# Graph convolution with split adjacency: all four chunks of adj and adjT split, none multiplied whole

## The reference

```python
HW = einsum('bnf,rfo->rbno', h, W[:, :F]) + einsum('rd,rdo->ro', W_edges, W[:, F:])[:, None, None, :]
A = stack([A1, A2, shifted, A1^T, A2^T, shifted^T, eye])   # A1 = A2 = adj
AHW = einsum('rbnm,rbmo->rbno', A, HW)
out = x + max(AHW, axis=0) + b
```

## Time and profile before

| what | us |
|---|---|
| median of 3 runs | 216.8 |
| lowest, highest | 215.47, 218.54 |
| the profiled execution, its own time | 217.13 |
| its span on the core | 215.1 |
| PE busy (matmuls, as modelled) | 205.6 |
| DVE busy | 176.9 |
| ACT busy | 161.2 |
| POOL busy | 89.0 |

### The profile page before, as it was taken

One profiled execution on the slowest core, in us unless ns is written; L12 is line 12 of the kernel. 1 busy time (PEld: TensorE's weight loads), 2 busy tenths in 40 slices (PEclk: granted clock), 3 DMA queues, 4 the chain that ended last, 5 costly groups with the idle time before them and its releaser, 6 DMA issues.

```text
span 215.1 us, 3407 instructions
## 1 busy us (share of the span) xinstructions
PE 205.6 (96%) x900; PEld 148.9 (69%) x900; DVE 176.9 (82%) x416; ACT 161.2 (75%) x433; POOL 89.0 (41%) x140
## 2 busy tenths in 40 slices
PE   7998699999999999999999999999999999999992
PEld 7456367767767777777767767776777777777771
DVE  3485987999889797988979798888979798897755
ACT  3888919897896969698796969689696969876230
POOL 3042633627252542726163452725254372726200
PEclk9999969999999999999999999999999999999999
DMA  6999999797595959789494968859395958824101
GB/s 182 307 347 376 365 320 257 167 362 197 192 369 141 387 102 355 222 265 318 158 388 84 402 148 317 267 195 369 101 406 121 375 146 257 279 98 52 50 0 49
DMA packets 33747, 51.06 MB, mean 237 GB/s; under 512 B 1873, under 2 KB 11329, under 8 KB 33729
## 3 DMA queue, kind: packets, MB, share of 16 engines
q1 hardware_dynamic: 31152, 46.53, 62.5%
q0 software_dynamic: 2304, 4.20, 11.9%
q10 hardware_dynamic: 272, 0.13, 0.2%
HBM read 46.65 MB, written 4.19 MB: 236 GB/s over the span
## 4 chain that ended last, share of the span: by engine, by line
PE 78%; DVE 8%; DMA 5%; SPq 4%; issue 2%; ACT 1%; DVEq 0%; ACTq 0%
PE bank_p L816 11%; PE bank_p L818 9%; PE bank_p L817 9%; PE bank_g L776 6%; PE bank_gT L755 5%; DMA x_sb<-in_x_dram 5%; PE bank_g L780 5%; PE bank_g L781 5%; PE bank_g L787 5%; PE bank_gT L767 4%; PE bank_gT L761 4%; PE bank_gT L760 4%; DVE best L613 3%; PE bank_p L806 3%; PE bank_p L716 3%; PE bank_p L724 3%
## 5 line engine op out<-in xcount | busy, mean ns | idle before, releaser
L323 POOL TENSOR_TENSOR a_lo<-adj_sb,a_hi 128x512 fp32r<-128x512 f32 x15 | 19.5, 1303 | 66.7 <-DVE h_lo L582 57.7
L613 DVE TENSOR_TENSOR best<-bank_p,best 128x512 f32<-128x512 f32 x48 | 33.2, 691 | 8.0 <-PE bank_p L818 6.9
L610 DVE SCALAR_TENSOR_TENSOR best<-bank_p,c_col,best 128x512 f32<-128x512 f32 x32 | 24.0, 750 | 9.2 <-ACT best L457 8.7
L438 ACT ACTIVATE gT_hi<-bank_gT 128x512 fp32r<-128x512 f32 x16 | 9.5, 594 | 28.8 <-PE bank_gT L767 28.3
L393 ACT ACTIVATE a_hi<-adj_sb 128x512 fp32r<-128x512 f32 x45 | 27.7, 621 | 0.0
L406 ACT ACTIVATE aT_hi<-adjT_sb 128x512 fp32r<-128x512 f32 x45 | 27.7, 621 | 0.0
L422 ACT ACTIVATE h<-x_sb,shift,rstd 128x128 f32<-128x128 f32 x60 | 24.7, 489 | 1.1 <-DVE shift L562 1.1
L780 PE MATMUL bank_g<-aT_hi,h_hi 128*128 128x512 f32 x45 | 24.4, 543 | 0.0
L576 DVE TENSOR_TENSOR aT_lo<-adjT_sb,aT_hi 128x512 fp32r<-128x512 f32 x30 | 24.1, 841 | 0.0
L760 PE MATMUL bank_gT<-a_hi,h_hi 128*128 128x512 f32 x45 | 23.6, 525 | 0.0
L309 POOL DMA_DIRECT2D x_bias<-in_xT_dram x16 | 13.9, 872 | 23.2 <-DMA x_bias<-in_biasT_dram 23.2
(11 more groups left out here) (118 smaller groups left out, 510.4 us busy)
## 6 DMA issues: line engine op xcount, KB each, us to landing
adj_sb<-in_adj_dram SPq DMA_DIRECT2D x15, 1024.0 KB, 5.7
adjT_sb<-in_adjT_dram SPq DMA_DIRECT2D x15, 1024.0 KB, 6.4
x_bias<-in_biasT_dram SPq DMA_DIRECT2D x16, 256.0 KB, 5.9
x_bias<-in_xT_dram POOLq DMA_DIRECT2D x16, 256.0 KB, 4.8
x_sb<-in_x_dram SPq DMA_DIRECT2D x15, 256.0 KB, 7.8
out_dram<-o_sb SPq DMA_DIRECT2D x15, 256.0 KB, 5.8
adj_sb<-in_adj_dram SPq DMA_DIRECT2D x4, 256.0 KB, 5.6
adjT_sb<-in_adjT_dram SPq DMA_DIRECT2D x4, 256.0 KB, 5.4
```

The costliest lines, as they stand in the source:

```text
L613: op = nc.vector.tensor_tensor(best[q][:, :], product, best[q][:, :], ALU.max)
```

## The change

All four chunks of both directions are split. The constants `WHOLE` and `SPLIT` go; VectorE makes the low parts of chunks 0 and 1 (`ND` = 2), GpSimd those of chunks 2 and 3 (`NG` = 2). The tiles a_hi, a_lo, aT_hi, aT_lo, h_hi, h_lo have four chunks in place of three; `summed` is one tile in place of two and is written in round 0 only. ScalarE copies chunks 0 to 3 in order, each to its high tile. TensorE issues four passes high by high, then four with h_lo, then four with a_lo. Waits on `sums_ready` for later rounds become waits on `ahi_ready` and `aThi_ready`.

```diff
-WHOLE = (0,)
-SPLIT = (1, 2, 3)
-NS = len(SPLIT)
-ND = NS - 1
+ND = 2
+NG = 2
+NS = ND + NG
...
             def part_sums(b):
-                pool.wait_ge(sums_ready, 2 * b + 2)
+                if b == 0:
+                    pool.wait_ge(sums_ready, 2)
+                else:
+                    pool.wait_ge(ahi_ready, b * NS)
+                    pool.wait_ge(aThi_ready, b * NS)
...
             def split_adj_last(b):
-                pool.wait_ge(ahi_ready, b * NS)
-                nc.gpsimd.tensor_tensor(a_lo[q][:, ND, :], adj_sb[q][:, C - 1, :], a_hi[q][:, ND, :].bitcast(F32),
-                                        ALU.subtract).then_inc(alo_last_ready, 1)
+                for c in range(ND, NS):
+                    pool.wait_ge(ahi_ready, (b - 1) * NS + c + 1)
+                    nc.gpsimd.tensor_tensor(a_lo[q][:, c, :], adj_sb[q][:, c, :], a_hi[q][:, c, :].bitcast(F32),
+                                            ALU.subtract).then_inc(alo_last_ready, 1)
...
             def split_adj(b):
-                for i, c in enumerate(SPLIT):
-                    nc.scalar.activation(a_hi[q][:, i, :], adj_sb[q][:, c, :], ACT.Copy,
-                                         accum_out=sums[q][:, 0, c:c + 1]).then_inc(ahi_ready, 1)
-                for c in WHOLE:
-                    last = nc.scalar.activation(summed[q][:, 0, c, :], adj_sb[q][:, c, :], ACT.Copy,
+                for c in range(C):
+                    last = nc.scalar.activation(a_hi[q][:, c, :], adj_sb[q][:, c, :], ACT.Copy,
                                                 accum_out=sums[q][:, 0, c:c + 1])
-                last.then_inc(sums_ready, 1)
+                    last.then_inc(ahi_ready, 1)
...
-                nc.scalar.activation(h_hi[q][:, :, :], h[q][:, SPLIT[0]:, :], ACT.Copy).then_inc(hhi_ready, 1)
+                nc.scalar.activation(h_hi[q][:, :, :], h[q][:, :, :], ACT.Copy).then_inc(hhi_ready, 1)
...
             def aggregate(b):
                 q = b % 2
-                pe.wait_ge(adjT_in[q], times(b))
                 pe.wait_ge(best_done, b * NBEST)
-                for c in WHOLE:
-                    nc.tensor.matmul(bank_g[:, 0:N], h[q][:, c, :], adjT_sb[q][:, c, :],
-                                     start=(c == WHOLE[0]), stop=False)
-                for i in range(NS):
-                    pe.wait_ge(aThi_ready, (b - 1) * NS + i + 1)
-                    nc.tensor.matmul(bank_g[:, 0:N], h_hi[q][:, i, :], aT_hi[q][:, i, :], start=False, stop=False)
-                    nc.tensor.matmul(bank_g[:, 0:N], h_lo[q][:, i, :], aT_hi[q][:, i, :], start=False, stop=False)
...
+                for c in range(C):
+                    pe.wait_ge(aThi_ready, (b - 1) * NS + c + 1)
+                    nc.tensor.matmul(bank_g[:, 0:N], h_hi[q][:, c, :], aT_hi[q][:, c, :], start=(c == 0), stop=False)
+                for c in range(C):
+                    nc.tensor.matmul(bank_g[:, 0:N], h_lo[q][:, c, :], aT_hi[q][:, c, :], start=False, stop=False)
...
```

More of the change, by code:

```diff
@@ L36, in gnn_kernel @@
     C = N // P
-    assert F == P and O == P and N == C * P and N <= 512 and C * GROUP == P and R == NPROD and B % 2 == 0 and B >= 4
+    assert F == P and O == P and C == NS and N == C * P and N <= 512 and C * GROUP == P and R == NPROD and B % 2 == 0 and B >= 4
     HALF = C // 2
@@ L71, in gnn_kernel @@
         aT_lo = pair("aT_lo", [P, NS, N], F32R)
-        summed = pair("summed", [P, 2, C, N], mybir.dt.bfloat16)
+        summed = sb("summed", [P, 2, C, N], mybir.dt.bfloat16)
         hT_hi = sb("hT_hi", [P, N], F32R)
@@ L404, in split_adjT @@
                     act.wait_ge(g_psum, b - 1)
-                for i, c in enumerate(SPLIT):
-                    nc.scalar.activation(aT_hi[q][:, i, :], adjT_sb[q][:, c, :], ACT.Copy,
-                                         accum_out=sums[q][:, 1, c:c + 1]).then_inc(aThi_ready, 1)
-                for c in WHOLE:
-                    last = nc.scalar.activation(summed[q][:, 1, c, :], adjT_sb[q][:, c, :], ACT.Copy,
+                for c in range(C):
+                    last = nc.scalar.activation(aT_hi[q][:, c, :], adjT_sb[q][:, c, :], ACT.Copy,
                                                 accum_out=sums[q][:, 1, c:c + 1])
-                last.then_inc(sums_ready, 1)
+                    last.then_inc(aThi_ready, 1)
             def make_h(b):
@@ L481, in _ @@
                 act.wait_ge(adj0_in[c], 16)
-                last = nc.scalar.activation(summed[0][:, 0, c, :], adj_sb[0][:, c, :], ACT.Copy,
+                last = nc.scalar.activation(summed[:, 0, c, :], adj_sb[0][:, c, :], ACT.Copy,
                                             accum_out=sums[0][:, 0, c:c + 1])
@@ L566, in split_adj_lo @@
                 q = b % 2
-                for i, c in enumerate(SPLIT[:ND]):
-                    dve.wait_ge(ahi_ready, (b - 1) * NS + i + 1)
-                    nc.vector.tensor_tensor(a_lo[q][:, i, :], adj_sb[q][:, c, :], a_hi[q][:, i, :].bitcast(F32),
+                for c in range(ND):
+                    dve.wait_ge(ahi_ready, (b - 1) * NS + c + 1)
+                    nc.vector.tensor_tensor(a_lo[q][:, c, :], adj_sb[q][:, c, :], a_hi[q][:, c, :].bitcast(F32),
                                             ALU.subtract).then_inc(alo_ready, 1)
@@ L573, in split_adjT_lo @@
                 q = b % 2
-                for i, c in enumerate(SPLIT[:ND]):
-                    dve.wait_ge(aThi_ready, (b - 1) * NS + i + 1)
-                    nc.vector.tensor_tensor(aT_lo[q][:, i, :], adjT_sb[q][:, c, :], aT_hi[q][:, i, :].bitcast(F32),
+                for c in range(ND):
+                    dve.wait_ge(aThi_ready, (b - 1) * NS + c + 1)
+                    nc.vector.tensor_tensor(aT_lo[q][:, c, :], adjT_sb[q][:, c, :], aT_hi[q][:, c, :].bitcast(F32),
                                             ALU.subtract).then_inc(aTlo_ready, 1)
@@ L581, in split_h_lo @@
                 dve.wait_ge(hhi_ready, b)
-                nc.vector.tensor_tensor(h_lo[q][:, :, :], h[q][:, SPLIT[0]:, :], h_hi[q][:, :, :].bitcast(F32),
+                nc.vector.tensor_tensor(h_lo[q][:, :, :], h[q][:, :, :], h_hi[q][:, :, :].bitcast(F32),
                                         ALU.subtract).then_inc(hlo_ready, 1)
@@ L750, in aggregate_T @@
                 q = b % 2
-                pe.wait_ge(h_ready, b + 1)
-                pe.wait_ge(adj_in[q], times(b))
+                pe.wait_ge(hhi_ready, b)
                 pe.wait_ge(gTlo_ready, b)
-                for c in WHOLE:
-                    nc.tensor.matmul(bank_gT[:, 0:N], h[q][:, c, :], adj_sb[q][:, c, :],
-                                     start=(c == WHOLE[0]), stop=False)
+                for c in range(C):
+                    pe.wait_ge(ahi_ready, (b - 1) * NS + c + 1)
+                    nc.tensor.matmul(bank_gT[:, 0:N], h_hi[q][:, c, :], a_hi[q][:, c, :], start=(c == 0), stop=False)
                 pe.wait_ge(hlo_ready, b)
-                for i in range(NS):
[L759 to L764, removed]
-                    else:
-                        pe.wait_ge(alo_last_ready, b)
-                    last = nc.tensor.matmul(bank_gT[:, 0:N], h_hi[q][:, i, :], a_lo[q][:, i, :],
-                                            start=False, stop=(i == NS - 1))
+                for c in range(C):
+                    nc.tensor.matmul(bank_gT[:, 0:N], h_lo[q][:, c, :], a_hi[q][:, c, :], start=False, stop=False)
+                for c in range(C):
+                    if c < ND:
+                        pe.wait_ge(alo_ready, (b - 1) * ND + c + 1)
+                    else:
+                        pe.wait_ge(alo_last_ready, (b - 1) * NG + c - ND + 1)
+                    last = nc.tensor.matmul(bank_gT[:, 0:N], h_hi[q][:, c, :], a_lo[q][:, c, :],
+                                            start=False, stop=(c == C - 1))
                 last.then_inc(gT_psum, 1)
```

34 lines of the change are left out of this document (17 added, 17 removed).

## The result

| | before | changed |
|---|---|---|
| median of 20 runs each, us | 216.14 | 218.09 |
| the profiled execution, us | 217.13 | 219.32 |
| its span, us | 215.1 | 217.6 |
| round 3 begins (first matmul of aggregate_T) | 50.98 | 53.24 |
| round 15 begins | 198.42 | 201.26 |

The ratio is 1.0066 (95% interval 1.0039 to 1.0094): slower by 0.7%, where 1.0% less was forecast. The time lies in the range, on the other side of no change. Two of the changed kernel's 20 executions stand far out (246.15 us, at a mean granted clock of 0.756, and 1106.65 us); the ratio is taken from the executions in the faster state alone. (The profiled execution of the changed kernel had 6.8 us at half the full clock in its start, the one before 3.4; the middle rounds of both ran at full clock.)

A forecast was written before the change was run, and what follows sets the result against it. TensorE, busy 96% of the span, was taken as the bound. From 217.13 us, -4.3 (13 batches), +0.95 (start) and +1.1 (caught batches) gave 214.9, or 214.6 for the median; range 212.0 to 220.6.

The forecast's parts named there:

- TensorE, -0.33 a round: Matrix passes: twelve split passes per direction replace one whole chunk and nine passes, 0.33 us less per batch, giving 11.95.
- The start, +0.95: Batches 1 and 2, not bound by TensorE: GpSimd's added subtractions and ScalarE's longer h_hi cost 0.95 us together.
- The tightest path: Middle batches: ScalarE's longer row stays hidden while VectorE's pair of aT_lo ends by 3.85 us into the batch.
- I take two of the twelve batches 3 to 14 as caught: GpSimd's finish gets between VectorE's two aT_lo in two middle batches, stalling TensorE 0.55 us each, +1.1 us.
- the second small subtraction: GpSimd's sums: expected 2.0 to 2.1 us into the batch, against VectorE's first aT_lo at 1.99, called close.
- the good side: Middle batches: small subtraction queues behind VectorE's first aT_lo, finish behind it again; the pair ends at 3.3 to 3.5 us.
- a caught batch doesn't shift the next one: Middle batches: after a hold, h_lo and GpSimd are late by as much as TensorE is, so the next batch is unaffected.
- Finish then falls beside work that reads PSUM: Middle batches: once VectorE's second aT_lo runs first, GpSimd's finish overlaps VectorE instructions reading PSUM, which do not suffer.
- slow rival: Finish gets between VectorE's two aT_lo in every batch, 0.55 us each: 220.1 us, chance 0.3 including mixtures from 216.8 up.
- Nothing collides: GpSimd and VectorE pass each other, in the start too, and all 15 batches gain: 211.8 us; chance of under 212.5: 0.2.
- GpSimd's loop as the bound: Finish, store, bias landing, bias add, two aT_lo and sums on GpSimd take about 12.0 us a batch; chance 0.05.

The follow-up runs named there:

- e1: Changed kernel with GpSimd's finish (add of best and x_bias) on 32 of 512 columns only, other output columns zero; 212.94 us, ratio 0.9856.
- e8: Changed kernel with VectorE's shift before its aT_lo, maximum 2 of round 0 before a_lo(1), and GpSimd's finish before the sums; 213.33 us, ratio 0.9864.
- e7: Changed kernel with GpSimd's finish(b) moved ahead of part_sums(b+1), to start before VectorE's first aT_lo; 214.99 us, ratio 0.9946.
- e5: Changed kernel with VectorE's shift ahead of its aT_lo and, in the start, maximum 2 of round 0 ahead of its two a_lo(1); 212.38 us, ratio 0.9809.
- e2: Changed kernel with VectorE's scale_and_shift(b+1) moved ahead of its two aT_lo(b) in rounds 2 to 14; 213.58 us, ratio 0.9884.
- e3: Control: the kernel before the change, with VectorE's shift moved ahead of its aT_lo; ratio 0.9952.
- e4: Changed kernel with VectorE making three low parts per direction and GpSimd one, in place of two each; 219.27 us, ratio 1.0132.

## Why the prediction was wrong

- **TensorE, -0.33 a round: right.** Wherever nothing stalls (e1, e8) a round is 11.93, against 11.95 worked out.
- **The start, +0.95: right in size.** e1, with the same single half-clock stretch as the kernel before, begins round 3 at 52.05, 1.07 later. The parts came out otherwise: round 1 is 0.65 us longer, where 0.25 was left for it, and round 2 0.42, where 0.5 and 0.14 stood, so the good sum is in part luck. The profiled changed kernel has a second such stretch on top.
- **The tightest path, pair of aT_lo, shift, h, sumsT, product 2: right.** The chain has it word for word, with its limit: the round grew by 0.46 us when h began 0.9 late.
- **"I take two of the twelve batches 3 to 14 as caught: 2 x 0.55": this is the step that failed.** Nine were caught and two more paid by the shift. At 11.93 the twelve would have taken 143.2 us and they took 148.0: +4.9 in place of +1.1. It failed in two places. First the phase: the second small subtraction came 1.86 us after the start of the round (2.02 after its first matmul, which the timeline has 0.16 before T 0), not at 2.0 to 2.1. The rival had named that very condition, GpSimd 0.15 us earlier than reckoned. A margin of 0.1 us in a sum of eight terms was no ground for taking the good side. Nor are the rounds independent, as "a caught batch doesn't shift the next one" has it. In e1, where a hold costs no time, the phase moves from round to round, and finish fell between the two aT_lo in five of rounds 3 to 13. In the changed kernel a caught round makes h_lo, and GpSimd's a_lo behind it, 0.92 us late and TensorE only 0.46; GpSimd then no longer waits for the bias, where it waited 0.4 to 0.6 in e1, and the second small subtraction comes at 2.01 to 2.03 us after the first matmul in every caught round. That a caught round so leads to the next one fits these numbers; no run tests it alone. Second, the good side wasn't free. "Finish then falls beside work that reads PSUM" overlooked the shift, which reads two small tiles in SBUF and stands between the pair and gT_lo. Round 7 (12.24 us) was on the good side and stalled 0.31 us. With that seen, both sides stall, the good one by 0.3 us, and the forecast lies near the slow rival's.
- **The slow rival: right in mechanism, 220.1 worked out, 218.1 measured.** The stall is 0.46 us a round in nine rounds and 0.3 in two, where it was priced at 0.55 in all twelve.
- **"Nothing collides": wrong.** Its 211.8 us was not reached, but its middle rounds are, by order alone: in e8 instructions are held in every round, where nobody waits, and the rounds take 11.93. **GpSimd's loop as the bound: not seen;** e1 and e8 have the four subtractions and 11.93.
- The hold is an exclusive lock, which the first to issue gets, as the Trainium skill, SBUF — State Buffer, section "Who interferes with whom" states it. The middle rounds agree (the pair takes 1.76 us in e7 and 2.35 in the changed kernel), and what waits may be as small as 128x4 (1.05 us in place of 0.16). The five stretches of e7 and e8 do not: there VectorE's instruction was issued before finish and ran after it.

What the change brings and what it costs, then: -0.36 us in each of 13 rounds (-4.7) against +4.9 of holds and +1.1 in the start give +1.3 us; the ratio of the runs, 0.0066 x 216.1, is 1.4. With the holds moved to where nobody waits and the start's move, the changed kernel is 1.9% under the kernel before (e5). That is not all the change's: with the shift first in both, it is 213.58 against 214.96 us (e2 and e3, medians of four), 0.6%. The start's move was not tried on the kernel before.

## What to carry to other kernels

When work goes to GpSimd, list every VectorE instruction with two inputs in SBUF, the tiny ones too, and ask which is followed by someone who waits; put those ahead of the large ones instead of counting on the phase. A collision that hangs on a tenth of a microsecond may come in nearly every round of a loop, since a caught round can set the phase of the next: price both sides, and don't take a small share of the rounds for the estimate. An idle share says nothing here, as GpSimd had 38% of the span left when it cost the time.

## What had not been expected of the hardware

A shift on 128x4 elements, 0.16 us of work, took 1.05 us while a GpSimd add of 128x512 had the port, and up to 1.79 us (e8, round 14) where a subtraction and the add of GpSimd ran one behind the other, although the add was issued after the shift. The clock in the start went its own way: the profiles up to e4 had one or two stretches of 3.4 us at half clock between 26 and 34 us, those of e5 to e8 none, and no run here says why. And the move that is neutral in the middle of the kernel before (e3) took 0.76 us off its round 2.
